# Scores of 16-wide heads as two float32r parts on 48 rows, two heads at once on the row halves, instead of three bfloat16 parts on 96 rows

## The chip, the cores and the metric

One core of one Trainium2 chip. The time is that of one execution on the device in microseconds (us).

## What is computed

Four transformer blocks with 16 heads follow each other on `x` of 32 elements x 256 tokens x 256 channels, with a context of 120 tokens for each element. Block 0: layer norm, causal self-attention, attention to the context, a gelu feed-forward of 1024. Block 1: self-attention with a key mask, attention to the context, a relu feed-forward of 1024, norms after the sums. Block 2: attention to the context with a mask of its own for each element. Block 3: attention to the context with heads 64 wide. Blocks 0 to 2 have heads 16 wide, and the change concerns these alone:

```python
scores = jnp.einsum('bqhd,bkhd->bhqk', qh, kh) / jnp.sqrt(jnp.float32(hd))
p = jax.nn.softmax(scores, axis=-1)
out = jnp.einsum('bhqk,bkhd->bqhd', p, vh)
```

## The kernel before

The kernel makes three passes over the 32 elements: "l0" is block 0, "l1" is block 1, "l2" is blocks 2 and 3 together. Between the passes x lies in DRAM. In a pass each engine follows a list written out by hand (`LISTS`, lines 58 to 243): a step such as `scores_max.own.2/0.81786` has a kind, an attention or stage ("own" is the first attention of a pass, "other" the second), a number, and a due time in periods of one element. `run` (line 396) adds the element's number to each due time (`Step`, with the small corrections of `SPREAD` for the first and last elements) and sorts; so each engine works on some five elements at a time, in one fixed order that is the same for every element in the middle of a pass. Every engine runs its order and waits on semaphores. `run` also deals out the eight PSUM banks by these due times.

An attention with heads 16 wide goes through these steps:

- `project_q`, `project_k` (line 1257): x or the context times the weights, in float32, into a bank.
- `split_hi` on ScalarE (line 762) rounds q or k to bfloat16, `split_rest` on VectorE (line 1002) takes the remainder, `split_mid` on ScalarE (line 780) rounds that, `split_lo` on GpSimd (line 695) takes what is left. So q and k are three bfloat16 parts.
- `spill` (line 537) writes each part to the slots of DRAM that need it (`Q_SLOTS`, `K_SLOTS`, lines 29 and 30: six pairs of parts), and `stack` (line 550) reads them back as 96 rows, 6 slots x 16, in `qstack` and `kstack`.
- `scores_max` (lines 1301 to 1324): a matmul per head and query tile, 96 rows deep, 256 or 128 or 120 keys wide; VectorE adds the mask and takes the row maximum (line 1046, line 1050). Its negative is split in three parts (`negate`, line 1066), turned by TensorE (`negate_t`, line 1325) and written by DMA as rows 97 to 99 of `qstack` (`nm_rows`).
- `scores_exp` (lines 1335 to 1364): scores again, keys by queries and 99 rows deep, with the maximum subtracted; the mask; exp on ScalarE.
- `probs_v` (line 1365): probabilities times v in float32, four heads at once, each in 32 columns of the array. `project_out` follows.

For one element pass l0 has 12 `scores_max` and 16 `scores_exp` jobs for "own" and 8 and 8 for "other", l1 has 16 and 16, 8 and 8, and l2 has 8 and 8. By their code they are these matmuls for an element: l0 48 of 256 columns, 32 of 128 and 32 of 120; l1 80 of 256 and 32 of 120; l2 16 of 256 and 32 of 120. All other matmuls have float32 operands, and each of those that is no transpose stands in the trace as two MATMUL instructions; a transpose is one. Block 3 has 64-wide heads: `scores3` (line 1419) puts two heads on the two row halves of the array, 64 rows each, in turn, and `probs_v3` two heads on 64 columns each.

Of the kernel before, what the change touches and what calls it, by code (L numbers as in the profile page):

```python
# [46 lines left out]
START = {"l0": 0.0, "l1": 33.12879, "l2": 66.18842}  # L47
# [13 lines left out]
            norm.0.0/0.24343 project_k.own.0/0.29714 project_q.own.0/0.33916 scores_max.own.2/0.81786 scores_max.own.8/0.82319  # L61
            scores_max.own.4/0.87055 scores_max.own.9/0.87589 scores_max.own.7/0.93916 scores_max.own.5/0.94449
            scores_max.own.6/0.94983 scores_max.own.1/0.96050 scores_max.own.3/1.01853 scores_max.own.0/1.02921
            scores_max.own.10/1.03455 scores_max.own.11/1.07681 negate_t.own.0/1.16618 project_k.other.0/1.16900
            project_v.own.0/1.20141 scores_exp.own.1/1.26914 scores_exp.own.6/1.27312 scores_exp.own.3/1.27715
# [1689 lines left out]
```

## Time and profile before

| | us |
|---|---|
| median of 3 runs | 4388.23 |
| the 3 runs | 4387.04, 4388.23, 4392.02 |
| span of the profiled execution | 4385.8 |
| the profiled execution's own time: not listed apart; the span lies below the fastest of the runs by | 1.2 |
| TensorE matmul busy | 4260.8 (97%), 33536 instructions |
| VectorE busy | 3663.2 (84%), 12709 |
| ScalarE busy | 2547.7 (58%), 6753 |
| GpSimd busy | 1590.0 (36%), 2709 |

PE is TensorE's matmul, PEld its weight load, DVE VectorE, ACT ScalarE, POOL GpSimd, SP SyncE. Matmuls are pipelined: the length of one in the profile (some 270 ns for a narrow one) is longer than the distance from its start to the next start, and it is that distance which fills the time. A timeline row gives the start of a group of like instructions, its length to the end of its last one, and its count; so the distance from the start of one row to the start of the next is the time that the group takes in the stream.

### The profile page before, as it was taken

The numbers are of one execution on the slowest core, as the hardware profiler recorded it, in microseconds if no ns is written. First come the engines' busy times: TensorE is split into PE (matmuls) and PEld (weight loads), VectorE is DVE, ScalarE is ACT, GpSimd is POOL, SyncE is SP. The second block draws the span as 40 slices with busy tenths as digits, with TensorE's granted clock in tenths as the row PEclk, the third lists the DMA queues.
The fourth block names the chain that finished last, engine by engine and source line by source line (L and its number), as shares of the span: only waits on it lengthen the run. The fifth ranks groups of instructions, "written<-read, shape, count | busy, mean of one in ns | idle before, by whom it ended". The sixth has DMA issues, their size and how long they took to land. (4 is left out here: it accounts for less than half of the span.)

```text
span 4385.8 us, 99261 instructions
## 1 busy us (share of the span) xinstructions
PE 4260.8 (97%) x33536; PEld 3436.5 (78%) x33536; DVE 3663.2 (84%) x12709; ACT 2547.7 (58%) x6753; POOL 1590.0 (36%) x2709
## 2 busy tenths in 40 slices
PE   5999999999999899999999999999999999999998
PEld 3788888888887677777777777778888888888886
DVE  4899999999997899999999999967777777777774
ACT  2556656566565545455454554536676767676765
POOL 3445454454452234444444444431222222222222
PEclk8999999999999999999999999999999999999999
DMA  5555455554553544545444454433222222222220
GB/s 172 147 154 161 133 151 153 140 161 138 149 157 114 152 132 137 141 127 163 133 146 132 133 149 124 135 98 84 62 78 61 79 61 79 61 77 63 72 66 9
DMA packets 406443, 513.40 MB, mean 117 GB/s; under 512 B 133808, under 2 KB 373936, under 8 KB 384432
## 3 DMA queue, kind: packets, MB, share of 16 engines
q1 hardware_dynamic: 398544, 496.82, 39.7%
q10 hardware_dynamic: 7392, 10.24, 0.7%
q8 instruction: 268, 4.39, 0.4%
q14 instruction: 239, 1.96, 0.2%
HBM read 266.30 MB, written 236.72 MB: 115 GB/s over the span
## 5 line engine op out<-in xcount | busy, mean ns | idle before, releaser
L816 ACT ACTIVATE probs_own<-bank 128x384 f32<-128x384 f32 (+2 forms) x1280 | 644.6, 569 | 80.0 <-DVE bank L1065 41.7
L723 ACT ACTIVATE ht<-bank,columns_l 128x256 f32<-128x256 f32 x384 | 197.2, 569 | 729.4 <-PE bank L1242 726.3
L625 POOL TENSOR_SCALAR veps<-meanvar 128x2 f32<-128x2 f32 x256 | 63.9, 249 | 1357.1 <-DVE meanvar L966 1357.1
L1189 PE MATMUL bank<-ht,w_ff 128*128 128x256 f32 x2048 | 489.8, 382 | 2.7 <-ACT ht L723 1.6
L1189 PE MATMUL bank<-w_ff,ffh 128*128 128x256 f32 x2048 | 475.7, 380 | 0.0
L1046 DVE DVE_READ_ACCUMULATOR2_ANT nmf_own<- 128x1 f32 x3072 | 433.5, 141 | 0.0
L1189 PEld LDWEIGHTS bank<-w_ff,ffh 128*128 128x128 f32 x2048 | 378.7, 190 | 49.4 <-issue 1.2
L1046 DVE CUSTOM_DVE_ANT_0 bank<-bank,mask_rows 128x256 f32<-128x256 f32 x1024 | 398.8, 457 | 21.2 <-PE bank L1189 21.1
L1189 PEld LDWEIGHTS bank<-ht,w_ff 128*128 128x128 f32 x2048 | 369.6, 190 | 50.0 <-ACT ht L723 2.8
L1189 PE MATMUL bank<-kstack_own,qstack_own 96*128 96x256 bf16 (+2 forms) x3072 | 370.1, 248 | 27.2 <-DMA kstack_own<-k_parts 18.7
L881 ACT ACTIVATE probs_other<-bank,negmax 128x120 f32<-128x120 f32 x1024 | 356.6, 383 | 59.6 <-DVE negmax L1169 59.6
L816 ACT ACTIVATE probs_other<-bank 120x512 f32<-120x512 f32 x512 | 280.4, 608 | 143.1 <-PE bank L1189 142.0
L1046 DVE CUSTOM_DVE_ANT_0 bank<-bank,causal_rows 128x256 f32<-128x256 f32 (+1 forms) x1024 | 326.8, 394 | 18.2 <-PE bank L1189 18.2
L1189 PEld LDWEIGHTS bank<-kstack_own,qstack_own 96*128 96x128 bf16 x3072 | 249.1, 99 | 117.5 <-issue 38.6
L1065 DVE TENSOR_TENSOR bank<-bank,mask_less 128x512 f32<-128x512 f32 x512 | 319.4, 686 | 15.3 <-PE bank L1189 11.2
L1189 PE MATMUL bank<-qstack_own,kstack_own 99*128 99x256 bf16 (+2 forms) x2560 | 303.8, 263 | 6.1 <-ACT probs_own L816 3.2
L1189 PE MATMUL bank<-ht,w_own 128*128 128x256 f32 x1280 | 302.6, 384 | 5.2 <-ACT ht L723 2.5
L1050 DVE TENSOR_REDUCE nmf_other<-bank 128x4 f32<-128x480 f32 x512 | 300.4, 633 | 2.9 <-PE bank L1189 2.9
L1189 PEld LDWEIGHTS bank<-qstack_own,kstack_own 99*128 99x128 bf16 (+1 forms) x2560 | 231.5, 105 | 90.7 <-issue 26.1
L1189 PE MATMUL bank<-probs_own,v_aug_own 128*32 128x256 f32 (+2 forms) x5120 | 286.2, 363 | 12.9 <-POOL probs_own L693 8.9
L1046 DVE CUSTOM_DVE_ANT_0 bank<-bank,m_rows 128x120 f32<-128x120 f32 x1024 | 255.0, 317 | 51.3 <-PE bank L1189 51.3
L705 POOL TENSOR_TENSOR q_parts_own<-remains_own,q_parts_own 128x256 bf16<-128x256 f32 x192 | 124.9, 671 | 401.2 <-issue 401.2
(164 smaller groups left out, 10138.4 us busy)
## 6 DMA issues: line engine op xcount, KB each, us to landing
qstack_own<-q_parts SPq DMA_DIRECT2D x96, 768.0 KB, 5.7
kstack_own<-k_parts SPq DMA_DIRECT2D x64, 768.0 KB, 7.3
qstack_other<-q_parts SPq DMA_DIRECT2D x64, 768.0 KB, 5.9
q_parts<-q_parts_own SPq DMA_DIRECT2D x96, 384.0 KB, 2.5
q_parts<-q_parts_own SPq DMA_DIRECT2D x96, 256.0 KB, 2.3
k_parts<-k_parts_own SPq DMA_DIRECT2D x64, 384.0 KB, 2.9
q_parts<-other_parts SPq DMA_DIRECT2D x64, 384.0 KB, 2.5
other_words<-k_parts SPq DMA_DIRECT2D x64, 360.0 KB, 3.3
```

Of the source, the lines that this page charges most:

```text
L625: nc.gpsimd.tensor_scalar(veps[key][:, :], meanvar[key][:, :, 1], r["norms"][key]["eps"], None, ALU.add).then_inc(veps_ready.sem, 1)
L705: ins = nc.gpsimd.tensor_tensor(f3[2][:, f, :], x32[:, f, :], f3[1][:, f, :], ALU.subtract)
L723: return nc.scalar.activation(out, in_, ACT.Identity, scale=scale, bias=bias)
L816: nc.scalar.activation(probs[key][0:rows, j % a.slots, 0:n], bank_of(u)[0:rows, 0:n], ACT.Exp, scale=a.scale).then_inc(a_done.sem, 1)
L881: ins = nc.scalar.activation(probs3[:, j % 4, n, :], bank[:, n * S2:(n + 1) * S2], ACT.Exp, scale=-1.0, bias=negmax3[:, j, n:n + 1], accum ...
L1046: ins = v.tensor_tensor_reduce(scores, scores, add, -1.0, LIMIT if a.masked == "each" else 3.0e38, ALU.add, ALU.min, nmf[key][:, t, at:at ...
L1050: ins = v.tensor_reduce(nmf[key][:, t, first:first + FT * len(heads) - FT + 1:FT], bank[:, 0:len(heads) * nk].rearrange("p (h k) -> p h k" ...
L1065: v.tensor_tensor(p, p, add, ALU.add).then_inc(masked_by_dve.sem, 1)
L1189: return nc.tensor.matmul(out, lhsT, rhs, start=first, stop=True, skip_group_check=True)
```

## The change

q and k are now two parts (`PARTS = 2`): the value rounded to float32r, and the rest. Three slots of 16 make 48 rows; the two row halves of the array (rows 0 to 47 and 64 to 111) hold heads of even and odd number, and every `scores_max` and `scores_exp` works on two banks, alternating between the halves. `split_mid` and GpSimd's `split_lo` go, `split_lo` is now VectorE's; the negated maximum has two parts and 2 `negate` steps instead of 4, and its transposes are float32. `stack` and `nm_rows` are two DMAs each; the stacks hold float32, 3 slots instead of 6 with elements twice as wide, so the same bytes. The weights of block 3's q are copied once from DRAM to DRAM. The masks stay on the engines where they were. All lists are new, and `SPREAD` is all zeros and ones.

```diff
-PARTS = 3
-Q_SLOTS = (0, 0, 0, 1, 2, 1)
-K_SLOTS = (2, 1, 0, 0, 0, 1)
+PARTS = 2
+HF = H // FT
+Q_SLOTS = (0, 0, 1)
+K_SLOTS = (0, 1, 0)
...
-START = {"l0": 0.0, "l1": 33.12879, "l2": 66.18842}
+START = {"l0": 0.00000, "l1": 33.20642, "l2": 66.01348}
...
+def place(h):
+
+    return h % FT, h // FT
+
+
+def tile_rows(f, n):
+    return slice(f * P // FT, f * P // FT + n)
...
                 if bias is None:
-                    ins = v.tensor_tensor(x32, src, hi, ALU.subtract)
+                    ins = v.tensor_tensor(lo.bitcast(F32R), src, hi, ALU.subtract)
...
             elif kind == "scores_max":
+
+                if j % 2:
+                    continue
...
-                for n, h in enumerate(heads):
-                    ins = mm(bank[:, n * nk:(n + 1) * nk], qstack[key][0:KS, stack_place(h), t * P:(t + 1) * P],
-                             r["kstack"][key][0:KS, stack_place(h), 0:nk], n == 0)
+                two = [take(u), take(plan["PE"][n_u + 1])]
                 n = len(heads)
+                for i in range(n):
+                    for f in range(FT):
+                        at = heads[i] // FT
+                        ins = mm(two[f][:, i * nk:(i + 1) * nk], qstack[key][tile_rows(f, KS), at, t * P:(t + 1) * P].bitcast(F32R),
+                                 r["kstack"][key][tile_rows(f, KS), at, 0:nk].bitcast(F32R), i == 0)
...
             elif kind == "negate_t":
-                    ins = nc.tensor.transpose(bank[0:2 * PARTS * H, t * P // 2:(t + 1) * P // 2].bitcast(BF16),
-                                              parts[:, t * PARTS * H:(t + 2) * PARTS * H], identb[:, :])
+                    ins = nc.tensor.transpose(bank[0:3 * PARTS * H, t * P:(t + 1) * P],
+                                              parts[:, t * PARTS * H:(t + 3) * PARTS * H], ident[:, :])
...
             elif kind == "scores_exp":
+                def part(f, at, out, keys, queries, first):
+                    kq = tile_rows(f, KS + PARTS)
+                    return mm(out, ks[kq, at, keys].bitcast(F32R), qs[kq, at, queries].bitcast(F32R), first)
+
                 if a.cross:
-                    for n, h in enumerate(heads):
-                        ins = mm(bank[0:S2, n * T:(n + 1) * T], ks[kq, stack_place(h), :], qs[kq, stack_place(h), :], n == 0)
+                    for n in range(2):
+                        for f in range(FT):
+                            ins = part(f, a.exp_heads(j)[n] // FT, two[f][0:S2, n * T:(n + 1) * T], slice(0, S2), slice(0, T), n == 0)
```

TensorE's list is the part of `LISTS` on which most hangs. That of pass l1, before and after (for an element in the middle of a pass the order is that of the due times' fractions, round and round):

```diff
-            turn.0.0/0.09548 project_q.own.0/0.13496 project_k.own.0/0.21530 scores_max.own.10/0.73194
-            scores_max.own.1/0.73685 scores_max.own.4/0.74177 scores_max.own.6/0.74668 scores_max.own.8/0.82894
-            scores_max.own.0/0.88226 scores_max.own.9/0.88717 scores_max.own.15/0.89467 scores_max.own.12/0.91892
-            scores_max.own.7/0.92384 scores_max.own.3/0.96742 project_v.own.0/0.97233 scores_max.own.13/1.03684
-            scores_max.own.5/1.04805 scores_max.own.14/1.05390 scores_max.own.11/1.06935 scores_max.own.2/1.07427
-            project_k.other.0/1.10521 negate_t.own.0/1.17403 scores_exp.own.1/1.25397 scores_exp.own.2/1.25888
-            scores_exp.own.7/1.26379 scores_exp.own.3/1.26871 scores_exp.own.0/1.27362 scores_exp.own.5/1.27853
-            scores_exp.own.6/1.36503 scores_exp.own.10/1.36995 scores_exp.own.12/1.37486 scores_exp.own.11/1.37977
-            scores_exp.own.4/1.38468 scores_exp.own.9/1.38959 scores_exp.own.8/1.39451 probs_v.own.0/1.44021
-            probs_v.own.1/1.45955 scores_exp.own.15/1.48101 scores_exp.own.13/1.48592 scores_exp.own.14/1.49083
-            probs_v.own.2/1.56548 probs_v.own.3/1.58482 project_out.own.0/1.83385 norm.1.0/2.12522 project_q.other.0/2.17662
-            scores_max.other.5/2.53442 scores_max.other.6/2.53924 scores_max.other.7/2.54407 scores_max.other.3/2.54889
-            scores_max.other.4/2.55371 scores_max.other.1/2.55854 scores_max.other.0/2.60627 scores_max.other.2/2.64977
-            negate_t.other.0/2.89208 project_v.other.0/2.89959 scores_exp.other.4/3.01101 scores_exp.other.3/3.01592
-            scores_exp.other.2/3.02083 scores_exp.other.0/3.02575 scores_exp.other.6/3.04176 scores_exp.other.7/3.05881
-            scores_exp.other.1/3.08000 scores_exp.other.5/3.08802 probs_v.other.0/3.32424 probs_v.other.1/3.33391
-            probs_v.other.2/3.34357 probs_v.other.3/3.35324 project_out.other.0/3.61110 norm.2.0/3.87252 ff_in.ff.1/3.92875
-            ff_in.ff.2/4.28344 ff_in.ff.0/4.39942 ff_in.ff.3/4.49575 ff_out.ff.0/4.65459 ff_out.ff.1/4.69327
-            ff_out.ff.2/4.75159 ff_out.ff.3/4.79026
+            turn.0.0/0.32088 project_k.own.0/0.42992 project_q.own.0/0.55123 project_k.other.0/1.11896
+            project_v.own.0/1.14054 scores_max.own.2/1.18379 scores_max.own.3/1.18379 scores_max.own.6/1.18955
+            scores_max.own.7/1.18955 scores_max.own.12/1.29283 scores_max.own.13/1.29283 scores_max.own.0/1.37516
+            scores_max.own.1/1.37516 scores_max.own.8/1.42417 scores_max.own.9/1.42417 scores_max.own.14/1.48420
+            scores_max.own.15/1.48420 scores_max.own.4/1.53594 scores_max.own.5/1.53594 scores_max.own.10/1.54169
+            scores_max.own.11/1.54169 negate_t.own.0/1.67341 scores_exp.own.2/1.74963 scores_exp.own.3/1.74963
+            scores_exp.own.6/1.76224 scores_exp.own.7/1.76224 scores_exp.own.4/1.76799 scores_exp.own.5/1.76799
+            scores_exp.own.0/1.81700 scores_exp.own.1/1.81700 scores_exp.own.10/1.85749 scores_exp.own.11/1.85749
+            scores_exp.own.14/1.90650 scores_exp.own.15/1.90650 probs_v.own.0/1.91225 scores_exp.own.8/1.92395
+            scores_exp.own.9/1.92395 probs_v.own.1/1.92971 scores_exp.own.12/1.95320 scores_exp.own.13/1.95320
+            probs_v.own.2/2.02522 probs_v.own.3/2.04100 project_out.own.0/2.23855 norm.1.0/2.47317 project_q.other.0/2.61762
+            project_v.other.0/2.83002 scores_max.other.4/3.00221 scores_max.other.5/3.00221 scores_max.other.0/3.01371
+            scores_max.other.1/3.01371 scores_max.other.6/3.05270 scores_max.other.7/3.05270 scores_max.other.2/3.10746
+            scores_max.other.3/3.10746 negate_t.other.0/3.29952 scores_exp.other.2/3.59449 scores_exp.other.3/3.59449
+            scores_exp.other.0/3.60508 scores_exp.other.1/3.60508 scores_exp.other.4/3.66087 scores_exp.other.5/3.66087
+            probs_v.other.0/3.67917 scores_exp.other.6/3.69130 scores_exp.other.7/3.69130 probs_v.other.1/3.69705
+            probs_v.other.2/3.75538 probs_v.other.3/3.85164 project_out.other.0/4.06421 norm.2.0/4.28180 ff_in.ff.2/4.33191
+            ff_in.ff.1/4.38092 ff_in.ff.0/4.49269 ff_in.ff.3/4.70290 ff_out.ff.0/4.77375 ff_out.ff.2/4.86325
+            ff_out.ff.1/4.95895 ff_out.ff.3/5.19530
```

The lists of l0 and l2 change in the same manner.

## Rows read from the trace of the kernel before

**Rows 1.** The view by stretches: start:end us, length, busy us of each engine, PEclk, DMA.
```profile
0.00:44.00 44.00, 12.71 (x60) 9.74 (x60) 11.43 (x61) 5.74 (x11) 12.66 (x27) 0.81 0.71 221
...
200.00:1300.00 1100.00, 1097.47 (x9104) 912.15 (x9102) 1011.17 (x3525) 697.31 (x1632) 521.60 (x939) 1.00 0.52 148
...
1550.00:2750.00 1200.00, 1195.00 (x9163) 943.51 (x9165) 1126.31 (x3653) 613.67 (x1301) 510.56 (x841) 1.00 0.48 138
...
3050.00:4250.00 1200.00, 1199.87 (x9529) 981.86 (x9528) 889.23 (x3379) 809.62 (x2709) 273.93 (x436) 1.00 0.25 70
```

**Rows 2.** The tile rec_own, written once an element, in the three middle stretches.
```profile
L1111 DVE RECIPROCAL rec_own<-ot_raw_own x26: 353/354/355, 226.7 to 1276.2; 128x32 f32<-128x32 f32 x26
...
L1111 DVE RECIPROCAL rec_own<-ot_raw_own x26: 330/333/334, 1582.0 to 2718.7; 128x32 f32<-128x32 f32 x26
...
L1111 DVE RECIPROCAL rec_own<-ot_raw_own x27: 353/353/354, 3066.2 to 4217.4; 128x32 f32<-128x32 f32 x27
```

**Rows 3.** TensorE's timeline in pass l1: start us, length us, instruction, count.
```profile
2003.50 0.60 PE L1189 MATMUL bank<-kstack_own,qstack_own 96*128 96x256 bf16 x4
2003.93 1.89 PE L1189 MATMUL bank<-ht,w_ff 128*128 128x256 f32 x8
2005.66 0.39 PE L1189 MATMUL bank<-kstack_own,qstack_own 96*128 96x256 bf16 x2
...
2022.21 1.93 PE L1189 MATMUL bank<-probs_other,other_words 120*32 120x256 f32 x32
2024.07 1.70 PE L1189 MATMUL bank<-qstack_own,kstack_own 99*128 99x256 bf16 x14
2025.61 1.89 PE L1189 MATMUL bank<-ht,w_ff 128*128 128x256 f32 x8
```

**Rows 4.** TensorE's timeline in pass l2.
```profile
3501.05 0.60 PE L1451 MATMUL bank<-ident,probs_other 128*120 128x128 f32 x4
3501.58 2.05 PE L1189 MATMUL bank<-vectors,probs_other 64*128 64x120 f32 x32
3503.56 1.95 PE L1189 MATMUL bank<-w_other,other_parts 120*64 120x256 f32 x16
3505.43 1.93 PE L1189 MATMUL bank<-probs_own,v_aug_own 120*32 120x256 f32 x32
3507.30 3.72 PE L1189 MATMUL bank<-w_ff,other_words 128*128 128x256 f32 x16
3510.86 1.94 PE L1189 MATMUL bank<-ct,ff_xu 128*128 128x120 f32 x16
3512.63 1.03 PE L1189 MATMUL bank<-w_own,ct 128*120 128x256 f32 x4
...
3519.60 0.60 PE L1451 MATMUL bank<-ident,probs_other 128*120 128x128 f32 x4
3520.03 0.58 PE L1189 MATMUL bank<-kstack_own,qstack_own 96*128 96x120 bf16 x8
3520.46 1.93 PE L1189 MATMUL bank<-w_v,ct 128*120 128x512 f32 x4
```

**Rows 5.** TensorE's timeline of two moments: the first pair and the first matmul of a stretch.
```profile
3501.58 0.37 PE L1189 MATMUL bank<-vectors,probs_other 64*128 64x120 f32 x2
...
3507.30 0.48 PE L1189 MATMUL bank<-w_ff,other_words 128*128 128x256 f32 x1
```

**Rows 6.** TensorE's groups by form: count, busy us, mean ns of one.
```profile
L1189 PE MATMUL bank<-kstack_own,qstack_own 96*128 96x256 bf16 x1536 | 245.5, 278 | 5.2 <-issue 3.1 <-DVE nmf_own L1046 1.3 <-ACT probs_other L816 0.4
...
L1189 PE MATMUL bank<-vectors,probs_other 64*128 64x120 f32 x2048 | 133.4, 280 | 0.0
```

**Rows 7.** VectorE's groups by form.
```profile
L1080 DVE TENSOR_TENSOR nmf_own<-nmf_own,nm_parts_own 128x32 f32<-128x32 f32 x96 | 18.4, 192 | 2.4
```

**Rows 8.** GpSimd's groups by form.
```profile
L705 POOL TENSOR_TENSOR q_parts_own<-remains_own,q_parts_own 128x256 bf16<-128x256 f32 x192 | 124.9, 671 | 401.2 <-issue 401.2
```

More of the change, by code:

```diff
@@ L10 @@
 BF16 = mybir.dt.bfloat16
+F32R = mybir.dt.float32r
 U8 = mybir.dt.uint8
@@ L60 @@
         "PE": """
[L61 to L65, printed above, removed]
@@ new lines @@
+            project_v.own.0/1.65569 scores_max.own.6/1.76773 scores_max.own.7/1.76773 scores_max.own.0/1.83210
+            scores_max.own.1/1.83210 scores_max.own.8/1.89699 scores_max.own.9/1.89699 negate_t.own.0/2.07921
+            scores_exp.own.6/2.15685 scores_exp.own.7/2.15685 scores_exp.own.2/2.16302 scores_exp.own.3/2.16302
+            scores_exp.own.0/2.16919 scores_exp.own.1/2.16919 project_k.other.0/2.17854 scores_exp.own.4/2.20168
+            scores_exp.own.5/2.20168 probs_v.own.0/2.25423 scores_exp.own.8/2.26400 scores_exp.own.9/2.26400
@@ new lines @@
+            scores_max.own.5/1.53483 scores_max.own.4/1.57815 scores_max.own.3/1.60661 scores_max.own.10/1.65865
+            scores_max.own.2/1.69649 scores_max.own.11/1.73114 scores_max.own.6/1.78436 scores_max.own.7/1.82925
+            project_v.own.0/1.86657 scores_max.own.1/1.89825 scores_max.own.0/1.93290 scores_max.own.9/1.96756
+            scores_max.own.8/1.98900 negate.own.0/2.03198 negate.own.1/2.07314 negate_t.own.0/2.09276 split_lo_k.other.0/2.25914
+            probs_v.own.0/2.33184 probs_v.own.1/2.56175 heads_rec.own.0/2.59959 heads_mul.own.0/2.64127 heads_back.own.0/2.68009
@@ new lines @@
+            project_out.own.0/2.76847 stats.1.0/2.80580 norm.1.0/2.88241 split_lo_q.other.0/3.09823 project_v.other.0/3.12443
+            scores_max.other.6/3.38562 scores_max.other.2/3.39912 scores_max.other.3/3.42845 scores_max.other.7/3.44195
+            scores_max.other.1/3.45545 scores_max.other.0/3.46894 scores_max.other.5/3.48244 scores_max.other.4/3.49594
+            negate.other.0/3.51098 negate.other.1/3.51573 negate_t.other.0/3.55628 probs_v.other.1/4.03519 probs_v.other.0/4.07635
@@ L181 @@
+            scores_max.other.2/3.19835 scores_max.other.3/3.21093 negate.other.0/3.25306 negate.other.1/3.27557
+            negate_t.other.0/3.31760 probs_v.other.0/3.74550 probs_v.other.1/3.89022 heads_rec.other.0/3.91913
+            heads_back.other.0/3.99377 project_out.other.0/4.12275 stats.2.0/4.15016 norm.2.0/4.22352 ff_out.ff.0/5.54980
+            stats.3.0/5.64711 norm.3.0/5.73074
         """,
         "POOL": """
-            split_lo_q.own.0/0.30381 split_lo_k.own.0/0.44689 xb.0.0/0.98571 heads_mul.own.0/1.66708 split_lo_k.other.0/1.69722
@@ L207 @@
[L207 to L211 removed]
+            turn.0.0/0.25047 project_q.own.0/0.31451 project_k.own.0/0.40675 scores_max.own.2/0.83080 scores_max.own.3/0.83080
@@ L221 @@
[L221 to L225 removed]
+            weights.k3.0/-29.61524 weights.v3.0/-17.00000 weights.own_qkv.0/-0.61652 turn.0.0/0.26499 split_hi_q.own.0/0.40502
@@ new lines @@
+            split_hi_k.own.0/0.43847 weights.own_o.0/0.48149 project_v2.own.0/1.06713 scores_exp.own.7/1.51417
+            scores_exp.own.5/1.52672 scores_exp.own.4/1.53928 scores_exp.own.3/1.57597 scores_exp.own.0/1.58906
+            scores_exp.own.6/1.60214 scores_exp.own.2/1.61523 scores_exp.own.1/1.62831 project_k3.three.0/1.80200
+            weights.q3.0/1.93424 project_k3.three.1/2.16915 norm.1.0/2.37058 project_v3.three.0/2.44515 project_q3.three.1/2.49224
+            project_q3.three.0/2.56098 scores3.three.2/2.64536 project_q3.three.3/2.68406 scores3.three.3/2.71279
@@ new lines @@
+            project_v3.three.1/2.75149 scores3.three.1/2.83928 scores3.three.0/2.87798 turn3.three.2/2.91668
+            project_q3.three.2/2.92889 weights.fc.0/2.94584 turn3.three.3/2.98058 scores3.three.7/2.98973 scores3.three.6/3.02843
+            turn3.three.0/3.08669 scores3.three.4/3.09583 turn3.three.1/3.19035 scores3.three.5/3.19949 probs_v3.three.1/3.39224
+            probs_v3.three.0/3.41654 turn3.three.6/3.42933 turn3.three.4/3.48309 turn3.three.7/3.50502 turn3.three.5/3.55183
+            probs_v3.three.2/3.70000 probs_v3.three.3/3.81410
@@ L486, in _ @@
         w = Where()
+        blanked = False
         for u in plan["SP"]:
@@ L617, in _ @@
             kind, key, j = u.tag
-            if not blank and kind != "stats":
+            if not blank and u is not plan["POOL"][0]:
                 blank = True
@@ L1066, in _ @@
             elif kind == "negate":
-                pt, f = nm_parts[key][:, 0:QT, :, :], nmf[key][:, :, :]
+                hi, lo = (nm_parts[key][:, 0:QT, :, i, :] for i in range(PARTS))
+                whole = nmf[key][:, :, :].rearrange("p t (f h) -> p t f h", f=FT)
                 if j == 0:
```

489 lines of the change are left out of this document (225 added, 264 removed), and 6 rows, old and new, of the table SPREAD.

## The prediction

> **What bounds the kernel now.** I read the busy shares first, then the view by stretches, then TensorE's timeline. The page gives TensorE 97% and VectorE 84%; what counts is the middle of each pass. There TensorE is busy 1097 of 1100 us, 1195 of 1200 and 1200 of 1200, at PEclk 1.00, the upper of its two levels (2.4 GHz); VectorE is busy for 92%, 94% and 74% [rows 1]. So TensorE's stream sets the pace, with VectorE close behind in l1. One element takes (1276.2 - 226.7)/25 = 42.0 us in l0, (2718.7 - 1582.0)/25 = 45.5 in l1 and (4217.4 - 3066.2)/26 = 44.3 in l2 [rows 2]. What I have to forecast is three periods, times 32 each.
>
> **The price list, as distances from start to start.** Eight float32 instructions of 256 columns take 1.73 us, 216 ns each; four bfloat16 score matmuls of 256 columns take 0.43, 109 ns each [rows 3]. A bfloat16 one of 120 columns takes 0.43/8 = 53 ns, a float32 instruction of 120 columns 1.77/16 = 111, a float32 transpose of 128 columns 0.43/4 = 109 [rows 4]; 56 for a bfloat16 one of 128 is the 120-column price by columns. probs_v issues four instructions on four column strips per 216 ns.
>
> **What row halves give, and what they cost.** scores3 is the model for the new scores: 32 instructions, 16 pairs on the two row halves, in 1.98 us; less the two surcharges below this is 1.78, 111 ns for a pair [rows 4, 6]. That is the price of one full-array instruction of the same size, so two halves do run at once. But the same rows show what a change of the array's shape costs. Four transposes take 0.43 us ahead of another full-array stretch and 0.53 ahead of scores3: 0.10 for leaving the shape. The first pair in the new shape is 0.37 long where all are 0.28 in the mean [rows 5, 6]: 0.095 more until the second can start. Back in the full array, 16 float32 instructions take 3.56 instead of 3.46 [rows 4]. The 16 of probs_v3 take 1.87 instead of 1.73, the 32 of probs_v 1.87 or 1.86 [rows 3, 4]. I take 0.095 us for each change of shape, and on entering 0.095 more in the full array with float32 and in row halves with float32, 0.04 on 64-column strips, 0.03 on 32-column ones, nothing before bfloat16 scores (14 of them after probs_v take 14 x 109 ns plus 0.01) [rows 3].
>
> The Trainium skill (TensorEngine Tiling, section Tiling Modes) says that changing the tiling mode, and not just the tile, drains the engine. By that rule, the trace agrees: it is the 0.10. The page's theoretical speedup for depths of 64 and less is up to 2x; by that alone, without the drains, scores would only gain, which is the second case below.
>
> **Part 1, the matmuls themselves.** Before, an element's scores cost: l0 48 x 109 + 32 x 55 + 32 x 53 = 8.7 us, l1 80 x 109 + 32 x 53 = 10.4, l2 16 x 109 + 32 x 53 = 3.4. After, they are 56, 56 and 24 pairs. No row shows float32r. A pair of 256 columns lies between 110 (a bfloat16 column rate) and 222 (a float32 instruction's rate); a pair of 120 or 128 columns between 56 and 111. For the wide ones I take 110, since one instruction with one part per operand is nearest to the bfloat16 row; the new lists place a wide pair of jobs 0.00575 apart and a float32 projection 0.04325, which is 0.230 us if the projection is 1.73, so whoever wrote the due times also reckoned 115 a pair. This is a hint, not a measurement. For the narrow ones I take 110 as well: transposes and narrow float32 instructions, with four-byte weights, do not go under 109 however few columns they have [rows 4]. Scores then cost 6.2, 6.2 and 2.6 us. negate_t's transposes go from 56 to 109 ns, four in l0 and l1 and two in l2: 0.2, 0.2 and 0.1 more. Net: -2.3, -4.0 and -0.7 us an element, 32 x 7.0 = 224 us less over the kernel.
>
> The Trainium skill (TensorE: Matmul & The Clock Gate, section LDWEIGHTS) gives a weight load as its columns over 1.2 GHz, 107 ns for 128; no run here shows it for float32r, and by it narrow pairs would cost 107, much as I take.
>
> **Part 2, changes of shape.** I went round the TensorE lists in the order of the due times' fractions and counted where neighbours differ in shape (full, row halves, 32 columns, 64 columns). Before, scores were full-array, so they sat beside projections at no cost: 6, 6 and 7 changes an element. After, score stretches are scattered through the list: 30, 41 and 29. Entered are 13 full, 11 row-half and 6 strip stretches in l0; 15, 19 and 7 in l1; 12, 10 (4 of scores3) and 7 in l2. Entering row halves with float32r is unmeasured: between 0.01 (bfloat16) and 0.095 (float32), I take 0.05. l0: 30 x 0.095 + 13 x 0.095 + 11 x 0.05 + 6 x 0.03 = 4.8, less 0.2 where a full stretch begins with transposes, which load faster; 4.6. l1: 3.9 + 1.4 + 0.95 + 0.2 - 0.2 = 6.25. l2 in the same way 4.4. Before, 0.7, 0.7 and 1.15. More by 3.9, 5.55 and 3.25 us: 32 x 12.7 = 406 us.
>
> **Part 3, waits of TensorE.** An l1 element is 14 float32 jobs of 8 (24.2), project_k of the context 0.9, project_v 0.9, 12 transposes 1.3, negate_t 0.2, 24 groups of probs_v 5.2, scores 10.4: 43.0; with 0.7 of changes 43.7, and 1.8 us are left for waits. The same sum leaves 0.85 in l0 (40.5) and 0.4 in l2 (42.7). After, l1 is 45.2 on TensorE against some 42.3 on VectorE (93.9% of 45.5, less a little), so waits shrink; I take 0.7 back in l1, 0.2 and 0.1 in the others: 32 us. The lists' ends are no better fitted than before (`SPREAD` is neutral), and the last DRAM copy of 1 MB runs in the first 44 us, where the DMAs move 221 GB/s [rows 1]: 0 to 9 us; I take 5 for all edges.
>
> **Part 4, edits at nothing.** GpSimd loses split_lo (671 ns each [rows 8]), ScalarE split_mid, VectorE two negate steps per attention (192 ns each [rows 7], for a negate_t copy that is a little longer). All of it lies under TensorE, which is busy over 99% of the middle; if that cover went, VectorE's share in l1 would be worth 0.35 us an element, 11 us. Spills and stacks move the same bytes; SP issues 20 DMAs for two attentions instead of 18, and they are a whole period ahead of need.
>
> **Sum.** -224 + 406 - 32 + 5 = +155 us against the profiled span of 4385.8, which is 2.4 under the median shown: 4388 + 155 = 4543, rounded to 4545, 3.6% slower.
>
> **The rivals.**
> - *Drains are covered or cheap* (faster). If a score stretch's start falls into a wait that is there anyway, or its weights are loaded ahead, part 2 shrinks. It decides at (224 + 32 - 5)/(32 x 81) = 0.10 us for each of the 81 changes added in a round of three elements, one of each pass, where I price 0.157 with the entry. At half my price the kernel takes 4388 - 251 + 203 = 4340; at none, 4137. For it: the new lists run further ahead (store at 5.4 to 6.7 periods where it was 4 to 5). Against it: TensorE waits in all for 3 us a round, so at most 96 us can be covered, and the surcharge appears in rows where nothing waits. Chance 0.17.
> - *Narrow pairs at the bfloat16 rate*: 32, 16 and 16 pairs at 56 instead of 110, 3.5 us a round of three elements: -111, 4434. Against it the 109 of transposes. Chance 0.12, nearly all on the slower side.
> - *float32r at half rate*: 72 wide pairs x 0.111 x 32 = +256, 4800. Chance 0.08.
> - *The halves do not overlap* (the change does not do what it says): 136 pairs x 0.108 x 32 = +470, 5015. scores3 speaks against it. Chance 0.03.
> - *The forecast*: 0.60, with its own range of 4430 to 4660 (entry 0.01 to 0.095 is 41 us either way, waits 30, prices of full stretches 40).
>
> **Numbers.** A measurement of this kernel can tell about 0.2%, 9 us, from no change. Faster: 0.17 and a little of the others' tails, 0.19. Within: 0.04. Slower: 0.77. The range of 4350 to 4690 leaves out about half of the first rival and the last two.
>
> **What would show it.** Right: in the profile after, a score stretch of wide pairs at 110 ns a pair, transposes or projections ahead of it 0.1 us longer than elsewhere, TensorE still over 99% busy in the middle with fewer matmul columns, periods of about 43.4, 46.3 and 46.8 us, VectorE's share down. Wrong: periods under the old ones (drains free), pairs at 220 (rate), narrow pairs at 56, or TensorE idle and waiting for VectorE or for DMAs (a misfit order, which I have not priced beyond the range).

## The result and the profile after

The kernel after takes 5213.2 us (5210.64 to 5218.38, 4 runs) against 4390.12 (4 runs of before beside it): 18.7% slower, ratio 1.1873, 95% interval 1.1857 to 1.189. The forecast was 4545, so the sign was right, and 668 us are missing from it. The profiled execution has a span of 5216.4 us. From its page:

```profile
PE 4709.0 (90%) x33536; PEld 3484.7 (67%) x33536; DVE 3658.1 (70%) x12389; ACT 2424.9 (46%) x6433; POOL 1202.8 (23%) x2071
...
PEclk7789888889888888999999999999999999999999
DMA  6445445544554445645555464555322332233221
GB/s 155 102 111 125 103 106 112 116 97 107 119 108 97 108 103 127 131 100 130 106 126 121 106 132 96 123 116 116 84 64 57 70 69 66 56 70 69 69 53 31
DMA packets 496224, 515.71 MB, mean 99 GB/s; under 512 B 133984, under 2 KB 408416, under 8 KB 495712
...
q1 hardware_dynamic: 488336, 499.18, 43.0%
```

TensorE is busy for 90% where it was 97%, and its granted clock stands at 0.7 to 0.9 in the first 16 of the 40 slices. The same queue in the kernel before:

```profile
q1 hardware_dynamic: 398544, 496.82, 39.7%
```

It took 43.0% of 5216 us, 2243 us, where 39.7% of 4386 was 1741: nearly the same megabytes in 29% more DMA time. The view by stretches, cut at 22 elements of each pass, as [rows 1] (length, busy us of PE, PEld, DVE, ACT and POOL, PEclk, DMA share, GB/s):

```profile
364.00:1623.00 1259.00, 1089.69 (x7657) 817.92 (x7657) 838.91 (x2860) 547.53 (x1276) 313.71 (x616) 0.89 0.49 109
2208.00:3395.00 1187.00, 1089.31 (x7658) 779.22 (x7657) 955.50 (x2949) 476.32 (x990) 330.51 (x528) 0.94 0.53 116
3920.00:4960.00 1040.00, 1036.77 (x7750) 785.91 (x7749) 713.85 (x2709) 640.60 (x2156) 176.04 (x264) 1.00 0.29 65
```

The tile `rec_own`, once an element, as [rows 2]; each window runs from element 6 to 28 of its pass:

```profile
L1086 DVE RECIPROCAL rec_own<-ot_raw_own x23: 347/348/351, 363.6 to 1622.8; 128x32 f32<-128x32 f32 x23
...
L1086 DVE RECIPROCAL rec_own<-ot_raw_own x23: 330/332/334, 2208.1 to 3395.1; 128x32 f32<-128x32 f32 x23
...
L1086 DVE RECIPROCAL rec_own<-ot_raw_own x23: 352/353/355, 3920.1 to 4959.7; 128x32 f32<-128x32 f32 x23
```

An element takes 1259.2/22 = 57.2 us in l0, 1187.0/22 = 54.0 in l1 and 1039.6/22 = 47.25 in l2. Forecast were 43.4, 46.3 and 46.8. So l2 is nearly right, and l0 and l1 are wrong by 13.8 and 7.7 us an element. The same two passes have a mean granted clock under 1 (0.89, 0.94), and TensorE is idle for 7.7 and 4.4 us an element. The list of TensorE's waits (us in total, times, longest):

```profile
PE bank L1164 <- DMA qstack_own<-q_parts: 162.2, 36, 26.3
PE bank L1164 <- DMA ct<-in_ctx: 107.8, 31, 5.4
PE bank L1164 <- DMA qstack_other<-q_parts: 74.1, 39, 3.8
PE bank L1164 <- DMA qstack_own<-nm_t_own: 55.0, 50, 5.6
```

All four are transfers: the stack of q for "own", the context, the stack of q for "other", and the rows of the negated maximum. One element of l0 on TensorE's timeline (start, length, instruction, count, the idle time before it):

```profile
1027.48 1.99 PE L1164 MATMUL bank<-w_ff,ffh 128*128 128x256 f32 x8
1031.61 1.55 PE L1164 MATMUL bank<-kstack_other,qstack_other 48*128 48x120 f32 x24 [2.13 <-DMA qstack_other<-q_parts]
1033.09 3.15 PE L1164 MATMUL bank<-w_ff,ffh 128*128 128x256 f32 x8
...
1037.68 1.99 PE L1164 MATMUL bank<-w_ff,ffh 128*128 128x256 f32 x8
1039.60 0.86 PE L1164 MATMUL bank<-probs_own,v_aug_own 128*32 128x256 f32 x16
1044.40 1.22 PE L1164 MATMUL bank<-kstack_own,qstack_own 48*128 48x256 f32 x8 [3.94 <-DMA qstack_own<-q_parts]
...
1046.14 1.51 PE L1164 MATMUL bank<-probs_own,v_aug_own 128*32 128x256 f32 x16
1047.58 1.11 PE L1164 MATMUL bank<-kstack_own,qstack_own 48*128 48x128 f32 x8
1048.62 6.49 PE L1164 MATMUL bank<-ht,w_ff 128*128 128x256 f32 x16
1054.95 1.89 PE L1164 MATMUL bank<-w_own,ht 128*128 128x256 f32 x8
```

and SyncE's issues in the same stretch:

```profile
1023.96 1.20 SPq L562 DMA_DIRECT2D qstack_other<-q_parts  x2
1025.28 0.54 SPq L544 DMA_DIRECT2D k_parts<-k_parts_own  x1
1025.86 0.44 SPq L544 DMA_DIRECT2D q_parts<-q_parts_own  x1
1026.49 0.37 SPq L544 DMA_DIRECT2D k_parts<-other_parts  x1
1031.99 1.20 SPq L562 DMA_DIRECT2D kstack_own<-k_parts  x2
1033.37 1.20 SPq L562 DMA_DIRECT2D qstack_own<-q_parts  x2
```

The stack of k for "own" waits for a spill that was issued at 1025.3, right behind the stack of q for "other", and goes out at 1032.0, 5.2 us after the last `scores_exp`; the stack of q follows at 1033.4, and the scores that need it start at 1044.4, after 3.94 us of waiting. In slices of 10 us:

```profile
1020.00:1030.00 10.00, 8.73 (x87) 6.41 (x84) 7.55 (x20) 7.95 (x20) 6.16 (x13) 1.00 0.94 182
1030.00:1040.00 10.00, 8.39 (x60) 6.66 (x64) 6.22 (x13) 1.05 (x3) 4.46 (x10) 0.83 1.01 193
1040.00:1050.00 10.00, 6.06 (x53) 4.01 (x42) 3.96 (x17) 0.00 (x0) 1.40 (x2) 0.70 0.37 61
1050.00:1060.00 10.00, 10.00 (x46) 7.76 (x44) 5.13 (x25) 5.31 (x13) 0.00 (x0) 0.79 0.00 0
```

For 20 us the DMA engines are fully taken. TensorE waits, its granted clock falls to 0.83, 0.70 and 0.79 (each slice a mean of the two levels, 2.4 and 1.2 GHz), and 16 float32 instructions starting at 1048.62 take 6.33 us until the next start, where two groups of 8 took 3.46 in [rows 3]. So a late stack is paid for twice: as the wait, and as a slow stretch of projections behind it.

### The profile page after: what moved, and what is told of

It is laid out like the page before. It is cut to its first block and busy times, and to the rows that moved or that the text cites. A ratio compares the mean times of both kernels' runs of the same rounds, so it can differ in the third digit from the quotient of the medians.

```text
span 5216.4 us, 98642 instructions
## 1 busy us (share of the span) xinstructions
PE 4709.0 (90%) x33536; PEld 3484.7 (67%) x33536; DVE 3658.1 (70%) x12389; ACT 2424.9 (46%) x6433; POOL 1202.8 (23%) x2071
## 5 line engine op out<-in xcount | busy, mean ns | idle before, releaser
L1164 PE MATMUL bank<-w_ff,ffh 128*128 128x256 f32 x3072 | 799.9, 406 | 0.1
L1164 PEld LDWEIGHTS bank<-w_ff,ffh 128*128 128x128 f32 x3072 | 581.7, 198 | 110.8 <-issue 8.9
L627 POOL TENSOR_SCALAR veps<-meanvar 128x2 f32<-128x2 f32 x256 | 57.2, 224 | 2338.4 <-DVE meanvar L946 2338.4
L1164 PE MATMUL bank<-ht,w_ff 128*128 128x256 f32 x2048 | 561.6, 426 | 1.7 <-ACT ht L713 1.3
L1164 PE MATMUL bank<-kstack_own,qstack_own 48*128 48x256 f32 (+2 forms) x3072 | 323.3, 324 | 167.8 <-DMA qstack_own<-q_parts 162.2
L1025 DVE CUSTOM_DVE_ANT_0 bank<-bank,causal_rows 128x128 f32<-128x128 f32 (+1 forms) x1024 | 330.3, 382 | 170.0 <-PE bank L1164 170.0
L1164 PEld LDWEIGHTS bank<-kstack_own,qstack_own 48*128 48x128 f32 x3072 | 237.2, 209 | 290.1 <-issue 251.5
L695 POOL TENSOR_SCALAR_AFFINE_SELECT probs_own<-probs_own 128x256 f32<-128x256 f32 x512 | 225.9, 466 | 562.6 <-ACT probs_own L797 560.0
L670 POOL TENSOR_TENSOR xb<-xh,vectors_l 128x256 f32<-128x256 f32 x320 | 243.5, 782 | 382.9 <-issue 228.7
L1164 PE MATMUL bank<-qstack_own,kstack_own 50*128 50x256 f32 (+2 forms) x2560 | 258.2, 309 | 77.0 <-DMA qstack_own<-nm_t_own 55.0
L818 ACT ACTIVATE ff_xu<-bank,columns_l 128x256 f32<-128x256 f32 x256 | 122.3, 478 | 438.5 <-PE bank L1164 438.4
```

The source lines that it names most:

```text
L627: nc.gpsimd.tensor_scalar(veps[key][:, :], meanvar[key][:, :, 1], r["norms"][key]["eps"], None, ALU.add).then_inc(veps_ready.sem, 1)
L670: ins = nc.gpsimd.tensor_tensor(xb[key][:, t, :], xh[src][:, t, :], mul, ALU.mult)
L695: nc.gpsimd.affine_select(out=p, in_=p, compare_op=ALU.is_ge, fill=0.0, base=0, pattern=[[0, 2], [1, P]], channel_multiplier=-1).then_inc( ...
L818: nc.scalar.activation(ff_x[:, j % 2, f, :], src, ACT.Identity, bias=r["ff"]["b"][:, at])
L1025: ins = v.tensor_tensor_reduce(scores, scores, add, -1.0, LIMIT if a.masked == "each" else 3.0e38, ALU.add, ALU.min, nmf[key][:, t, at:at ...
L1164: return nc.tensor.matmul(out, lhsT, rhs, start=first, stop=True, skip_group_check=True)
```

## The experiments

The theories: **T**, the transfers of the stacks are late; **Q**, SyncE's queue is (number of DMAs, waits in line); **S**, TensorE's own stream is longer than I priced it. Ratios are to the kernel before on the same chip, with their 95% intervals. "After" is the kernel after the change, 5213.2 us. The edits are cut to what matters, and lines such as `q_scratch: (SLOTS, P, FT * T)` give the shape of a DRAM tensor in short form. e1, e8, e9 and e12 leave out three quarters of what spills and stacks move, so most of their scores come from old values; they are there for their time alone.

**e1_quarter_bytes.**

```diff
+few = FT * nt if u.element % NB == 0 else FT * nt // 4
-sp.dma_start(dst, src[:, j, None, :].broadcast_to(...))
+sp.dma_start(dst[:, :, 0:few], src[:, j, None, 0:few].broadcast_to(...))
...
+few = HF if u.element % NB == 0 else HF // 4
-    sp.dma_start(stack[tile_rows(f, KS), :, :], runs[f])
+    sp.dma_start(stack[tile_rows(f, KS), 0:few, :], runs[f][:, 0:few, :])
```

> The kernel after, from the second element of each pass on with only a quarter of each spill's columns and a quarter of each stack's heads moved (2 of 8 head places), same number of DMAs, same order, same waits; so most scores are computed from old values. Theory T (transfers): in l0 and l1 the spills and stacks, some 5.3 MB an element in bursts at 94 to 101% DMA share, land too late for scores_max, TensorE waits, and its granted clock falls. Then the periods, 57.5 and 54 us, fall to what was forecast for TensorE alone, 43.4 to 45 in l0 and 46.3 to 48 in l1, l2 stays at 47.2, and the whole takes 4550 to 4650 us. Theory Q (SyncE's queue: the number of DMAs, their issue time and the waits they stand behind, whatever the bytes): over 5000. Theory S (TensorE's own stream is slower in l0 and l1, by changes of shape or clock without any wait on a DMA): no change, 5213.

4666.95 us, 1.0633 (1.0617 to 1.0649): 546 us less. By stretches of 22 elements:

```profile
305.00:1311.00 1006.00, 967.23 (x7660) 737.21 (x7659) 832.14 (x2864) 546.66 (x1276) 313.64 (x616) 1.00 0.17 47
1824.00:2869.00 1045.00, 1034.70 (x7656) 738.20 (x7655) 966.63 (x2948) 475.68 (x990) 331.28 (x528) 1.00 0.16 46
3371.00:4410.00 1039.00, 1036.74 (x7750) 785.85 (x7749) 713.64 (x2707) 639.66 (x2156) 175.74 (x264) 1.00 0.11 29
```

Periods 45.7, 47.5 and 47.2 us at a clock of 1.00. T holds for 546 of the 668 missing; Q falls, since the DMAs, their order and their waits are all still there. The 122 left are taken up in the next section. TensorE's own timeline here gives the prices of part 2, undisturbed (pass l1):

```profile
2215.02 1.89 PE L1166 MATMUL bank<-ht,w_ff 128*128 128x256 f32 x8
2216.84 0.50 PE L1166 MATMUL bank<-kstack_own,qstack_own 48*128 48x256 f32 x4
2217.28 1.99 PE L1166 MATMUL bank<-ht,w_ff 128*128 128x256 f32 x8
2219.20 0.50 PE L1166 MATMUL bank<-kstack_own,qstack_own 48*128 48x256 f32 x4
2219.63 1.99 PE L1166 MATMUL bank<-ht,w_own 128*128 128x256 f32 x8
```

Eight float32 instructions between two score stretches take 1.92 us, not 1.73; a stretch of two wide pairs takes 0.43. By the medians of all such places in the trace, from start to start, the last float32 instruction before row halves takes 309 ns instead of 216 (0.093 for leaving), the first wide pair 223 instead of 118 (0.10 for entering), the first narrow one 161 instead of 112 (0.05), and the first float32 instruction after a score stretch 320 instead of 216 (0.104).

**e2_long_runs.**

```diff
-q_scratch: (SLOTS, P, FT * T)
+q_scratch: (FT, SLOTS, P, T)
-runs = r["scratch"][x, key].rearrange("n (d h) (f t) -> f (n d) h t", d=D, f=FT)
+runs = r["scratch"][x, key].rearrange("f n (d h) t -> f (n d) h t", d=D)
```

> The kernel after with the DRAM scratch laid out by row half first, so that a row of a stack is one run of 8 KB (3840 B for 120 keys) as before the change, where it is now eight runs of 1 KB. Each spill is one DMA for each slot instead of one for each part, so SyncE issues 4 DMAs more for an attention. Order and bytes are the same. Theory T in the form 'the layout makes the transfers long': packets of 1 KB took 91 ns in the kernel after (11 B/ns), those of 8 KB 505 ns before (16 B/ns); the DMA work of an l0 element falls from 29 to some 22 us, and the time to 4750 to 4950 us. In the form 'the lists leave the stacks no room, whatever the layout': 5050 to 5200. Theory Q: slower than 5213, by some 4 x 0.4 us for each attention in l0 and l1, about 5300.

5119.06 us, 1.1668 (1.1647 to 1.1689): 94 less than after. That is the second version of T (5050 to 5200), in which the lists leave the stacks no room; the first (4750 to 4950) fails. Q fails again, with more DMAs and less time. Periods 55.4 and 53.1 in l0 and l1. The queue's line:

```profile
q1 hardware_dynamic: 401296, 499.20, 40.8%
```

2089 us of DMA time instead of 2243. But an 8 KB packet, a row of a stack, now takes 693 ns in the mean, where it took 505 before the change: the length of the runs is not all.

**e3_earlier_steps.**

```diff
-split_lo_q.own.0/1.13178 split_lo_k.own.0/1.16834   (l0, VectorE)
+split_lo_q.own.0/0.94500 split_lo_k.own.0/0.99500
-spill_k.own.1/1.18939 spill_q.own.1/1.19248 load_c.c.0/2.00308   (l0, SyncE)
+spill_q.own.1/0.99000 spill_k.own.1/1.03500 load_c.c.0/1.60000
-load_c.c.0/1.00288   (l1, SyncE)
+load_c.c.0/0.84000
```

> The kernel after with a few due times earlier: in l0 VectorE's split_lo_q and split_lo_k of own at 0.945 and 0.995 (were 1.132 and 1.168), their spills at 0.99 and 1.035 (1.192 and 1.189), so that SyncE's stacks of own wait for the last scores_exp alone, and load_c at 1.6 (2.003); in l1 load_c at 0.84 (1.003), ahead of the stack of k. Nothing else. If order is the cause: the wait for ct (107.8 us) goes, stacks of own in l0 are issued some 5 us sooner after the last scores_exp, l0's period falls to 48 to 52, l1's to 50 to 52, the whole to 4850 to 5000 us. If the transfers' own length is the cause and not the order: 5100 to 5213.

5090.99 us, 1.1605 (1.1587 to 1.1622): 122 less, just short of the version "transfers alone" (5100 to 5213) and well above "order alone". l0 falls to 52.2, just above the 48 to 52 expected; l1 does not fall (54.7, after has 54.0). The wait for the context is gone from l1, and this one has taken its place (in l1's 22 elements):

```profile
PE bank L1164 <- DMA qstack_own<-q_parts: 103.9, 22, 7.0
```

4.7 us an element for the stack of q, where the context had cost 3.8: moving a transfer forward moves the others back.

**e4_before_short_runs.**

```diff
-k_parts, q_parts: (SLOTS, P, FT * n)
+k_parts, q_parts: (SLOTS, P, 2, FT * n)[:, :, 0, :]
```

> The kernel before with its DRAM scratch padded, each row of 1 KB followed by 1 KB unused, so that its stacks read runs of 1 KB as in the kernel after, instead of 8 KB. Nothing else. If the short runs alone are what costs: over 2% slower, 4480 to 4700 us, with TensorE waiting for stacks. If they cost only together with the new lists, which leave less room between spill, stack and scores: within 0.5% of 4390, with the DMA share up from 0.52 to about 0.65 in l0 and TensorE still over 99% busy.

4402.74 us, 1.003 (1.0019 to 1.004). The queue's line:

```profile
q1 hardware_dynamic: 613584, 496.82, 42.0%
```

DMA time rises to 42.0% of 4400, 1848 us (+107), its share in l0 to 0.56, less than the 0.65 expected, and the order of before covers nearly all of it.

**e5_one_stack_dma**, e2's layout with one DMA for a stack over rows 0 to 111, rows 48 to 63 included.

```diff
-q_scratch: (FT, SLOTS, P, T)
+q_scratch: (FT, SLOTS + 1, P, T)
-for f in range(FT):
-    sp.dma_start(stack[tile_rows(f, KS), :, :], runs[f]).then_inc(...)
+rows = P // FT + KS
+sp.dma_start(stack[0:rows, :, :], runs[0:rows]).then_inc(...)
```

> As the kernel of the long runs, but a stack is one DMA over 112 rows instead of two over 48: the DRAM scratch has a fourth slot for each half (ones, written once), so rows 0 to 111 follow each other at one stride. 17% more bytes in the stacks. In the run with long runs the stacks still moved at 155 to 200 GB/s where the kernel before, with one DMA over 96 rows, moves 225 to 311, and its 8 KB packets took 693 ns instead of 505. If two DMAs over 48 rows, on the two halves, are what makes them slow: 8 KB packets back to about 520 ns, SyncE spends 0.35 us on a stack instead of 0.8 to 1.2, periods in l0 down from 55.5 by 3 to 6 us, the whole 4850 to 5000 us. If the slow rate is only several transfers at once: bytes decide, 5100 to 5200 us.

4919.43 us, 1.1191 (1.1153 to 1.123): 200 less than e2, although 7% more bytes move:

```profile
q1 hardware_dynamic: 401456, 534.95, 38.0%
```

1872 us instead of 2089, and 8 KB packets at 492 ns. **e6_one_stack_earlier** adds e3's due times.

> The one-DMA stacks together with the earlier steps of split_lo, spills and load_c of the third run. If room in the lists and the rate of the stacks both count, the gains add: some 100 us under the one-DMA kernel, 4750 to 4900 us. If the wait only moves on to the next late stack: no further gain, the same as the one-DMA kernel.

4772.95 us, 1.0875 (1.0854 to 1.0896): 146 less again, where the same edit gave 122 alone (e5's own runs lie between 4890 and 4929). Periods 47.5 and 50.2. Room and rate add.

**e7_before_two_stack_dmas** and **e14_before_interleaved_dmas.**

```diff
-sp.dma_start(stack[0:KS, :, :] ..., runs)
+for half in (slice(0, KS // 2), slice(KS // 2, KS)):      (e7)
+for half in (slice(0, KS, 2), slice(1, KS, 2)):           (e14)
+    sp.dma_start(stack[half, :, :] ..., runs[half])
```

> The kernel before with each stack as two DMAs of 48 rows (0 to 47, 48 to 95) instead of one of 96; bytes, runs of 8 KB and order are the same. If a DMA of 48 rows is slow by itself: 8 KB packets take about 690 ns instead of 505, DMA share in l0 up from 0.52 to 0.6, the time hardly changed by it (4387 to 4420) because the lists before leave room. If only the gap between the row halves, or the interleaving of two DMAs into the two halves, is slow: packets stay near 505 ns.

> The kernel before with each stack as two DMAs of 48 rows again, but one takes the even rows 0, 2, ... 94 and the other the odd rows, where the seventh run took 0 to 47 and 48 to 95. Bytes, runs of 8 KB, number of DMAs, rows in each DMA and order are those of the seventh run. The Trainium skill (SBUF, section on the DMA port swizzle) gives each row a port by its number: rows 0 to 47 lie on 8 of the 16 ports, 48 to 95 on 12, every second row on all 16. If the ports are what made two narrow DMAs slow: 8 KB packets fall from 623 ns back to about 505 to 530, the queue's share from 43.6% to about 40%. If it is the number of DMAs or of rows in each: 623 ns and 43.6% as in the seventh run. The time stays at 4387 to 4405 us in either case, since the lists before leave room.

4396.94 us, 1.0012 (1.0002 to 1.0021), and 4387.93 us, 0.9997 (0.9988 to 1.0007). The queue's lines, e7 and then e14:

```profile
q1 hardware_dynamic: 403664, 496.84, 43.6%
```

```profile
q1 hardware_dynamic: 403664, 496.84, 39.0%
```

The 8 KB packets take 623 ns in e7 and 492 in e14, with the same rows per DMA, the same number of DMAs and the same bytes. So neither the number of DMAs nor 48 rows in each is slow by itself; which rows a DMA takes is. A row of the stack is also a run in DRAM, and e14 alternates both, so no run separates the rows of SBUF from the places in DRAM that they are read from. The Trainium skill (SBUF — State Buffer, section Door 1: The DMA port swizzle) says that a transfer's rate depends on how many of the 16 ports its partitions reach, that bit 6 of the partition number chooses one of a pair of ports, and that adding 32 changes nothing. Worked out by that rule, rows 0 to 47 reach 8 ports, and so do rows 64 to 111; rows 48 to 95 reach 12, rows 0 to 95 or every second one of them 16. The measured order agrees: 693 ns for 8 and 8 ports (e2), 623 for 8 and 12 (e7), 492 and 505 for 16 (e14 and the kernel before). The ports themselves stand in no trace here.

**e8_grouped_scores** and **e9_light_grouping**, on e1.

```diff
-scores_max.own.0/1.37516 scores_exp.own.8/1.92395 project_q.other.0/2.61762
+scores_max.own.0/1.29300 scores_exp.own.8/1.90700 project_q.other.0/2.59300   (e8, l1; 32 steps in all)
-project_out3.three.0/3.56312 scores_max.own.2/0.83080 turn.0.0/0.25047
+project_out3.three.0/3.55150 scores_max.own.2/0.80000 turn.0.0/0.22800   (e9, l2; 22 steps in all)
```

> The kernel with a quarter of the bytes (scores mostly from old values, as in the first run), and TensorE's lists of l0 and l1 with neighbouring score and probs_v stretches drawn together: changes of shape 30 to 25 in l0 (3 full and 2 row-half stretches fewer), 41 to 28 in l1 (7 row-half, 4 full, 2 strips fewer), l2 as it was. Matmuls the same. At 0.094 us for leaving a shape and 0.10 for entering (read from the first run): l0 45.6 to 44.6, l1 47.5 to 45.1, l2 47.2, the whole 4667 to about 4560 us. If changes cost nothing or are hidden: 4667. If drawing them together makes TensorE wait for banks instead: over 4667, with waits for ScalarE or VectorE in the list of waits.

> The kernel with a quarter of the bytes (scores mostly from old values), and TensorE's lists changed where a stretch can be joined to its neighbour by moving a step less than 0.07 of a period, without more than six banks in one stretch of scores: changes of shape 30 to 27 in l0, 41 to 34 in l1, 29 to 20 in l2 (the fuller grouping of the eighth run made TensorE wait for ScalarE, so this one is lighter). Matmuls the same. At 0.094 us for each shape left and 0.05 to 0.104 for each entered, read from the first run: l0 45.6 to 45.05, l1 47.5 to 46.3, l2 47.2 to 45.8, the whole 4667 to about 4570 us. If changes cost nothing that is not hidden: 4667 and l2 at 47.2. If banks run short again: longer, with waits for ScalarE or VectorE.

4892.25 us, 1.1157 (1.1129 to 1.1185), and 4744.14 us, 1.0807 (1.0791 to 1.0823): both slower than e1, by 225 and 77. The third case of each text: TensorE waits for banks that ScalarE has yet to read (its waits for ScalarE's `probs_own` come to 75.4 us in e8 and 115.5 in e9, 28.8 in e1). e9's loss lies in l1, where the period goes from 47.5 to 50.1 us with 1.8 of such waits an element, and the joins of l1 are not told apart. In e9's l2, over 22 elements, and the one place that waits:

```profile
3442.00:4483.00 1041.00, 1010.43 (x7756) 791.32 (x7752) 711.31 (x2709) 631.85 (x2157) 176.13 (x265) 1.00 0.11 29
```

```profile
3715.79 0.72 PE L1166 MATMUL bank<-qstack_own,kstack_own 50*120 50x256 f32 x8
3717.80 1.16 PE L1166 MATMUL bank<-vectors,probs_other 64*128 64x120 f32 x16 [1.29 <-ACT probs_own L799]
```

TensorE's busy time falls from 47.1 to 1010.43/22 = 45.9 us an element, as the 9 changes should give, and 1.29 us comes back ahead of a `scores3` stretch that now follows the last `scores_exp` directly.

**e12_quarter_few_joins** keeps only the joins that brought no wait.

```diff
-turn.0.0/0.25047 scores_max.own.2/0.83080 project_v2.own.0/0.98772 probs_v.own.2/1.62725 probs_v.own.1/1.75155
+turn.0.0/0.22800 scores_max.own.2/0.80000 project_v2.own.0/0.97600 probs_v.own.2/1.69600 probs_v.own.1/1.70180   (l2)
```

> The kernel with a quarter of the bytes, with only those joins of stretches that brought no wait in the ninth run: changes of shape 30 to 28 in l0, 41 to 38 in l1, 29 to 22 in l2. In the ninth run l2's TensorE was busy for 1.2 us an element less but one scores3 stretch waited 1.29 us for a bank; that join is left out. If each change costs its 0.094 us and the entry 0.03 to 0.104: l2 47.2 to 46.2, l0 45.6 to 45.3, l1 47.5 to 47.0, the whole 4667 to about 4610 us. If l2 at 47.2 is held by another loop (stack, scores, negate, scores, exp) and not by TensorE: l2 stays at 47.2 and TensorE waits 1 us.

4627.64 us, 1.0545 (1.053 to 1.0561), 39 less than e1 where 57 were expected. The tile `rec_own` in l2, in e1 and in e12:

```profile
L1088 DVE RECIPROCAL rec_own<-ot_raw_own x23: 352/353/355, 3371.5 to 4410.1; 128x32 f32<-128x32 f32 x23
```

```profile
L1088 DVE RECIPROCAL rec_own<-ot_raw_own x23: 353/353/354, 3365.7 to 4379.1; 128x32 f32<-128x32 f32 x23
```

47.2 to (4379.1 - 3365.7)/22 = 46.06 us for 7 changes fewer, 0.16 each with the entry. l0 gives 0.3 as expected; l1 loses 0.3 to a wait for ScalarE.

**e10_queue_l1, e11_queue_and_grouping, e13_best_correct**, on e6.

```diff
-load_x.x.0/0.00000 spill_q.own.0/0.81316 stack_q.own.0/1.00575 spill_k.other.0/1.81029   (l1, SyncE)
+load_x.x.0/0.00700 spill_q.own.0/0.79900 stack_q.own.0/0.96400 spill_k.other.0/2.01100   (e10, e11; e13 without the last)
```

> The one-DMA stacks with the earlier steps (4773 us), and in l1 SyncE's steps reordered: own's spills of q ahead of the stack of q for other, own's two stacks directly after each other, load_x and the spills of k for other behind them. TensorE still waits 35 us in l1 for own's stack of q. If that wait is SyncE's order: l1's period from about 49.7 to 48 to 48.7, the whole 4715 to 4750 us. If the DMAs' rate is what is left: no change.

> All together, with every output right: one-DMA stacks, earlier steps, l1's SyncE order, and the light grouping. If the parts add: under the tenth run by about 90 us, 4630 to 4660. Both theories leave it slower than the kernel before by 5% or more, since TensorE's own stream alone is longer than before.

> One DMA for a stack, the earlier steps, in l1 SyncE's load_x behind the two stacks of own and the spills of q ahead of other's stack of q (the spills of k for other stay where they were, since moving them made VectorE late in the tenth run), and the few joins. All outputs right. If these effects add: 4773 less 60 for the joins less 20 to 60 for l1, 4650 to 4700 us, 6 to 7% over the kernel before. If the l1 reorder only moves the wait again: 4715 to 4780.

4850.9 us, 1.1048 (1.1029 to 1.1066): 78 slower than e6, a miss. The largest of TensorE's waits is new:

```profile
PE bank L1170 <- DVE other_parts L1002: 63.9, 29, 3.4
```

The spills of k, put later, hold up VectorE's `split_lo_k`, and with it a bank; in e13, where they stand as in e6, this wait is gone. e11, with e9's joins, is no better: 4857.99, 1.1071 (1.1051 to 1.1091). e13 takes out what had brought waits and has e12's joins: 4691.15 us, 1.0689 (1.0671 to 1.0707), 522 less than after with every byte moved, periods 46.5, 48.1 and 46.1. It does not beat the kernel before, and nothing here points to a version that does: e12, with the transfers all but gone, is still 5.5% slower.

## Why the forecast was wrong

- **The step that failed** stands in part 4: "Spills and stacks move the same bytes; SP issues 20 DMAs for two attentions instead of 18, and they are a whole period ahead of need." The bytes are the same; the rest of it is wrong, and it cost 546 us. (a) The two heads of a channel pair lie side by side in DRAM, so a row of a stack is eight runs of 1 KB instead of one of 8 KB. (b) The two DMAs each write 48 rows of one half of SBUF: 693 instead of 505 ns for 8 KB once (a) is undone. Undoing (a) takes 154 us of DMA time away (e2), undoing (b) 217 (e5). (c) "A period ahead" holds for the projections; the stack itself, in its single buffer, can start only when the last `scores_exp` of the element before is through, due 2.296 in l0, and `scores_max` is due at 1.522, 0.23 of a period later: about 10 us for 1.5 MB, which take 8 to 9.5 us at the 165 to 193 GB/s of the rows (an estimate), with nothing to spare for a late spill. I read the due times of the producers and not those of the buffer. Undoing all three in part (e6) brought 440 us back.
- **What the lateness cost**, from the rows: against e1, TensorE idles 5.95 us an element more in l0 and 4.0 in l1, and its busy time, for the same instructions, is 49.5 instead of 44.0 and 49.5 instead of 47.0. 32 x (11.5 + 6.4) = 574, against 546 measured. In l0 half of it is the clock. My text named idle TensorE as what would prove it wrong, "which I have not priced beyond the range": that was the price to work out.
- **Part 1 was right**: wide pairs are 118 ns (taken: 110), narrow ones 112 (110). At these prices float32r runs nearly at bfloat16's column rate (109 ns for 256 columns), two halves overlap, and narrow pairs do not halve. The three rivals on rates fall.
- **Part 2 was right in kind, some low in size**: 0.093 for leaving (0.095), but 0.10 for entering row halves with wide float32r (0.05) and 0.104 in the full array (0.095). The counts of changes are right (30, 41 and 29 in e1's trace). The growth of TensorE's stream is the test of parts 1 and 2: forecast were 1.6, 1.55 and 2.55 us an element, measured from before to e1 are 2.1 (41.9 to 44.0 busy), 1.75 (45.3 to 47.05) and 2.8 (44.3 to 47.1), 32 x 0.95 = some 31 us more. The measured prices would add 0.6, 1.3 and 0.25 to the forecast; that fits l0 and l2, and is 1.1 too much in l1, which stays open. That removing changes shortens the period is shown in l2, and in l0 by 0.3 us for two of them (e12).
- **Part 3** was wrong. "TensorE waits in all for 3 us a round" was what my sums left over; [rows 1] show TensorE idle for 0.1, 0.2 and 0.0 us an element. The 3 us stand there as busy: the price list was too low for the kernel before by as much, and since a matmul's length in the profile is longer than its share of the stream, short waits may hide in it; no run tells the two apart. So there was nothing to give back. With the transfers out of the way TensorE idles 1.75, 0.47 and 0.1 us an element, 66 us more than before where I took 32 off. The 1.75 in l0 is 1.0 us for the rows of the negated maximum, still a DMA, and 0.75 for ScalarE.
- **The drains rival** (faster) falls: with nearly all waits for transfers gone the kernel is still 6.3% slower, and the changes show in the period.

In sum: 4545 + 31 (stream) + 98 (waits) = 4674, measured 4667 in e1; + 546 (transfers) = 5213. Against my sums for TensorE after the change (42.8, 45.2 and 46.4 us) the stream of e1 is 1.2, 1.8 and 0.7 us too long; but the kernel before stood 0.7, 1.6 and 0.4 above its own sums, so most of that was there before the change.

## What to carry over

When a layout changes, write down for each DMA the length of its runs on both sides and which rows it writes, and weigh it against the time between the release of its buffer and its first reader, not its producer's lead. Two heads on the row halves pay only where score stretches are long: each stretch of wide pairs costs about 0.4 us in two changes of shape, and a wide pair saves 2 x 109 - 118 = 100 ns against two bfloat16 matmuls, so by this estimate a stretch needs about four of them to break even; narrow pairs (112 ns against 2 x 53) save nothing. l1 has 56 pairs in 19 stretches, 40 of them wide. Joining stretches costs PSUM banks, so count both. Where an order is already tight, price lateness twice: the wait, and the lower clock after it.
